# The second experts' rows in owner-sorted tiles of 128, with weights fetched by a register

## The reference, cut to what matters

```
x += norm(ssm + top1_experts(ssm))        # scan of 16 states; E=4 experts, 128 -> 512 -> 128, silu
x += cross_attention(norm(x), ctx)        # 256 queries, 256 keys per batch, one head of 128
# third block: top-2 of 8 experts, capacity 640 per expert
gates, idx = top_k(softmax(x @ wg), 2);  gates /= sum(gates)
loc  = cumsum(one_hot) - 1 (+ counts of first choices for second choices)
keep = loc < C;   pos = where(keep, idx * C + loc, E * C)
h = silu(disp @ fc1_w.T + fc1_b);  y = h @ fc2_w.T + fc2_b      # per expert
out = norm(x + gates[0] * y[pos0] + gates[1] * y[pos1]) * gamma + beta
```

## Time and profile before

| | |
|---|---|
| median of 3 runs | 476.78 us (476.72 to 478.07) |
| the profiled execution | 482.02 us |
| its span, first to last instruction | 480.2 us |
| mean granted TensorE clock | 0.885 |
| TensorE busy | 344.7 us (72% of the span) |
| VectorE, ScalarE, GpSimd busy | 292.0, 263.0, 230.6 us |
| DMA | 23.94 MB |

### The profile page before, as it was taken

One profiled execution on the slowest core, in us unless ns is written; L12 is line 12 of the kernel. 1 busy time (PEld: TensorE's weight loads), 2 busy tenths in 40 slices (PEclk: granted clock), 3 DMA queues, 4 the chain that ended last, 5 costly groups with the idle time before them and its releaser, 6 DMA issues. The chain is left out here.

```text
span 480.2 us, 5947 instructions
## 1 busy us (share of the span) xinstructions
PE 344.7 (72%) x1749; PEld 233.6 (49%) x1749; DVE 292.0 (61%) x840; ACT 263.0 (55%) x465; POOL 230.6 (48%) x275
## 2 busy tenths in 40 slices
PE   1427557769896899978999688661537789999460
PEld 0203333346464565645667455561327757767360
DVE  3478988956999799999974245357136012222055
ACT  3554645668887797868537675413224474554021
POOL 4425755543545665464541422716844435455434
PEclk9999965879999899999899988975558899999966
DMA  6999400000000000000000000200120221210243
GB/s 123 290 233 333 124 1 1 0 0 1 1 1 0 2 1 1 1 2 0 1 1 2 0 0 9 81 1 23 50 61 28 77 67 49 76 53 14 78 120 88
DMA packets 29472, 23.94 MB, mean 50 GB/s; under 512 B 5448, under 2 KB 23943, under 8 KB 29440
## 3 DMA queue, kind: packets, MB, share of 16 engines
q1 hardware_dynamic: 27048, 19.50, 14.8%
q0 software_dynamic: 2304, 4.04, 2.5%
q10 hardware_dynamic: 88, 0.03, 0.0%
HBM read 13.73 MB, written 10.52 MB: 51 GB/s over the span
## 5 line engine op out<-in xcount | busy, mean ns | idle before, releaser
L1072 POOL TENSOR_TENSOR yD<-yD,hc 128x512 f32<-128x512 f32 x64 | 84.4, 1318 | 103.5 <-DVE hc L537 97.9
L1398 PE MATMUL bank<-yD,w 128*128 128x512 f32 x128 | 71.9, 645 | 17.1 <-ACT hid L1202 16.2
L502 DVE TENSOR_TENSOR_SCAN h<-a,bank 128x512 f32<-128x512 f32 x64 | 77.8, 1216 | 1.4 <-DVE bank L489 0.5
L1407 PE MATMUL bank<-w,hid 128*128 128x128 f32 x512 | 74.6, 293 | 0.0
L1407 PEld LDWEIGHTS bank<-w,hid 128*128 128x128 f32 x512 | 68.6, 205 | 9.4 <-issue 6.1
L1389 PE MATMUL bank<-rows,selid 99*128 99x512 bf16 x128 | 47.5, 457 | 25.5 <-DVE hc L537 23.4
L1135 POOL DMA_INDIRECT y_rows<-yslot,dest x40 | 39.1, 977 | 37.6 <-DVE yslot L865 22.1
L1202 ACT ACTIVATE hid<-bank,cols 128x512 f32<-128x512 f32 x64 | 43.4, 683 | 18.0 <-PE bank L1398 11.9
L489 DVE TENSOR_TENSOR bank<-bank,u 128x512 f32<-128x512 f32 x64 | 43.8, 684 | 14.5 <-PE bank L1389 14.2
L1060 POOL DMA_INDIRECT slots_in<-xrow,posu x32 | 32.3, 1010 | 32.7 <-DVE locs L684 14.7
L1389 PEld LDWEIGHTS bank<-rows,selid 99*128 99x128 bf16 x128 | 12.8, 106 | 67.4 <-DVE hc L537 47.0
(11 more groups left out here) (235 smaller groups left out, 586.4 us busy)
## 6 DMA issues: line engine op xcount, KB each, us to landing
slots_in<-yslot SPq DMA_DIRECT2D x10, 258.0 KB, 6.3
xe_tok<-slots_in SPq DMA_DIRECT2D x8, 258.0 KB
y_rows<-yslot SPq DMA_DIRECT2D x8, 256.0 KB, 5.2
x_tok<-in_x_dram SPq DMA_DIRECT2D x4, 256.0 KB, 3.9
w<-in_L_attn_up_w_dram SPq DMA_DIRECT2D x1, 1024.0 KB
yD<-y_rows SPq DMA_DIRECT2D x4, 256.0 KB, 4.4
xT<-y_rows SPq DMA_DIRECT2D x4, 256.0 KB, 5.7
out_dram<-acc SPq DMA_DIRECT2D x4, 256.0 KB, 2.3
```

The source lines that it names most:

```text
L502: ins = v.tensor_tensor_scan(state_of(k), decay_of(k).rearrange("p j n -> p (j n)"), drive_of(k), 0.0, ALU.mult, ALU.add)
L1072: pool.tensor_tensor(grp(yD, g), grp(yD, g), read_of(k), ALU.add).then_inc(summed, 1)
L1398: pe.matmul(bank[UP_BANKS[f % 2]][:, 0:width(g)], w1[:, e, f * P:(f + 1) * P], grp(yD, g), start=True, stop=True).then_inc(up_ps, 1)
L1407: ins = pe.matmul(bank[DOWN_BANK][:, j * P:(j + 1) * P], hid[:, m % 2, f, j * P:(j + 1) * P], w2[:, e, f, :], start=(f == 0), stop=(f == F ...
```

## The change

The rows of the second experts no longer have fixed slots. They are sorted by expert into tiles of 128 rows, in three sets of tokens: token tiles 0 to 7, 8 to 11 and 12 to 15. A set of n token tiles has 2n + 7 row tiles, the most that eight experts can need, and all are computed: 23 + 15 + 15 = 53 row tiles. The first 38 run two per slot in slots 86 to 104, among the last group's attention steps; the last 15 after the slots.

- Weights: each expert's two transposed matrices are stored once to DRAM (`wts`, 8 x 512 KB, after they were turned at slot 14). For each row tile SyncE loads the owner's number into a register and fetches that owner's 512 KB into a ring of eight.
- VectorE: `seats` and `owners` work out where each expert's rows begin, and who owns each tile; `owners` also makes the tile's up bias. `take_in` copies four turned row tiles from PSUM to SBUF, `take_out` their four products. `combine` adds the two gated rows to the sum.
- GpSimd: 16 sends for the first set (slots 76 to 83), 8 for the second (slots 87 to 90), 8 for the third, after the slots; then 32 indirect gathers take each token's two result rows (`fetch`), of which the first eight stand at slot 99. The 40 sends to `y_rows` are gone.
- TensorE: per row tile one turn, four up products, one product over eight rows that adds the down bias of the owner, four down products. The gated sum is gone. ScalarE: four silus of 128x128 per tile.
- The loads of rows (`rows_in`), of weights and the stores of results (`rows_out`) are one queue of issues on SyncE, in the order that the diff shows.

```diff
+STAGES = 3
+BOUNDS = (0, 8, 12, TILES)
+MTS = [2 * (BOUNDS[s + 1] - BOUNDS[s]) + E2 - 1 for s in range(STAGES)]
+FFN_TILES = sum(MTS)
...
+W_RING = 8
+ROW_RING = 6
+Y_RING = 2
...
+FFN_SLOT = NS * G + 22
+FFN_PACE = 2
+def ffn_at(k):
+    n = FFN_PACE * (k - FFN_SLOT)
+    return [t for t in range(n, n + FFN_PACE) if 0 <= t < FIRST_TILE[-1]]
+def turns_at(k):
+    return [chunk_of(t) for t in ffn_at(k + 1) if t == chunk_tiles(chunk_of(t))[0]]
+def leaves_at(k):
+    return [chunk_of(t - 1) for t in ffn_at(k - 1) if t and t - 1 == chunk_tiles(chunk_of(t - 1))[-1]]
+FETCH_SLOT = FFN_SLOT + 13
...
+            def seats(g):
+                first, end = counted(g).start, counted(g).stop
+                square = [P, E2, E2]
+                link(v.tensor_tensor(firsts[:], off[:, end, 0, :], off[:, first, 0, :], ALU.subtract))
+                link(v.tensor_tensor(count2[:], off[:, end, 1, :], off[:, first, 1, :], ALU.subtract))
+                link(v.tensor_tensor(count2[:], count2[:], firsts[:], ALU.add))
+                link(v.tensor_tensor(full[:], count2[:].unsqueeze(2).to_broadcast(square),
+                                     rows128[:].unsqueeze(1).to_broadcast(square), ALU.is_gt))
+                link(v.tensor_reduce(tiles2[:], full[:], AX.X, ALU.add))
+                link(v.tensor_tensor(full[:], below[:], tiles2[:].unsqueeze(1).to_broadcast(square), ALU.mult))
+                link(v.tensor_reduce(lead2[:], full[:], AX.X, ALU.add))
+                for r in range(2):
+                    do(v.scalar_tensor_tensor(seat[:, r, :], lead2[:], float(P), off[:, first, r, :],
+                                              ALU.mult, ALU.subtract))
+                v.wait_ge(dve_done, n[0])
+                do(v.tensor_tensor(seat[:, 1, :], seat[:, 1, :], firsts[:], ALU.add))
+            def owners(s):
+                m = MTS[s]
+                mine = slice(FIRST_TILE[s], FIRST_TILE[s] + m)
+                wide = [P, m, E2]
+                link(v.tensor_tensor(past2[:], lead2[:], tiles2[:], ALU.add))
+                link(v.tensor_tensor(whose[:, 0:m, :], iota24[:, 0:m].unsqueeze(2).to_broadcast(wide),
+                                     past2[:].unsqueeze(1).to_broadcast(wide), ALU.is_ge))
...
+                link(v.tensor_copy(owner_no[:, mine], owner[0:1, 0:m]))
+                at["owner", s] = n[0]
+                do(v.tensor_scalar(owner_col[:, mine], owner[0:E2, 0:m], part_no[0:E2, 0:1], None, ALU.is_equal))
+                link(v.tensor_tensor(whose[:, 0:m, :], owner[:, 0:m].unsqueeze(2).to_broadcast(wide),
+                                     iota8.unsqueeze(1).to_broadcast(wide), ALU.is_equal))
+                link(v.tensor_tensor(bias_of[:, 0:m, :, :], whose[:, 0:m, :].unsqueeze(2).to_broadcast([P, m, FT, E2]),
+                                     cols[:, C_FCB:C_FCB + E2 * FT].rearrange("p (e f) -> p f e", f=FT)
+                                     .unsqueeze(1).to_broadcast([P, m, FT, E2]), ALU.mult))
+                link(v.tensor_reduce(up_bias[:, mine, :], bias_of[:, 0:m, :, :], AX.X, ALU.add))
+                at["up_bias", s] = n[0]
...
+            def take_in(c):
+                tiles = chunk_tiles(c)
+                v.wait_ge(xs_ps, c + 1)
+                if tiles[-1] >= XS_RING:
+                    v.wait_ge(up2_ps, tiles[-1] - XS_RING + 1)
+                for lo, hi in ring_runs(tiles, XS_RING):
...
+                at["xsT", c] = n[0]
+            def take_out(c):
+                tiles = chunk_tiles(c)
+                v.wait_ge(dn2_ps, tiles[-1] + 1)
+                if c >= Y_RING:
+                    v.wait_ge(st_y[c % Y_RING], 16 * (c // Y_RING))
+                else:
+                    v.wait_ge(zeroed, 16 * N_ZERO)
+                do(v.tensor_copy(yst[:, c % Y_RING, 0:len(tiles), :],
+                                 tiles3(bank[DOWN2_BANKS[c % 2]][:, 0:len(tiles) * P])))
+                at["yst", c] = n[0]
...
+            def combine(q):
+                v.wait_ge(acc_done, q + 1)
+                for i in range(q * GT, (q + 1) * GT):
+                    v.wait_ge(fetched[i], 32)
+                    for r, t in enumerate((first_y, second_y)):
+                        link(v.scalar_tensor_tensor(acc[:, i, :], t[:, i, :], g2[:, i, r:r + 1], acc[:, i, :],
+                                                    ALU.mult, ALU.add))
+                ln_stats(acc, quads(q), q, 4)
...
+            last = range(FIRST_CHUNK[-1], FIRST_CHUNK[-1] + CHUNKS[-1])
+            take_out(last[0] - 1)
+            combine(0)
+            take_in(last[0])
+            take_in(last[1])
+            combine(1)
+            take_in(last[2])
             finish(0)
-            sum_stats(3)
+            take_out(last[0])
+            take_in(last[3])
+            combine(2)
             finish(1)
+            take_out(last[1])
             finish(2)
+            take_out(last[2])
+            take_out(last[3])
             q = PG - 1
+            combine(q)
+            v.wait_ge(biased[3], G)
             for j in range(GT):
...
+            def weights(t):
+                r = t % W_RING
+                s = stage_of(t)
+                if t == FIRST_TILE[s]:
+                    sp.wait_ge(dve_done, at["owner", s])
+                if t == 0:
+                    sp.wait_ge(st_w, 16)
+                e = sp.value_load(owner_no[0:1, t:t + 1], min_val=0, max_val=E2 - 1)
+                if t >= W_RING:
+                    sp.wait_ge(dn2_ps, t - W_RING + 1)
+                load(wring[:, r, :], wts[bass.ds(e, 1), :, :].rearrange("e p n -> p (e n)"), ld_wt[r])
+            def rows_in(s):
+                sp.wait_ge(scattered[s], 16 * 2 * (BOUNDS[s + 1] - BOUNDS[s]))
+                for c in range(FIRST_CHUNK[s], FIRST_CHUNK[s] + CHUNKS[s]):
+                    tiles = chunk_tiles(c)
+                    first = tiles[0] - FIRST_TILE[s]
+                    if c >= ROW_RING:
+                        sp.wait_ge(xs_ps, c - ROW_RING + 1)
+                    load(xs_tok[:, c % ROW_RING, 0:len(tiles), :],
+                         srt[s][first * P:(first + len(tiles)) * P, :].rearrange("(j p) d -> p j d", p=P),
+                         ld_rows[c % ROW_RING])
+            def rows_out(c):
+                tiles = chunk_tiles(c)
...
+                sp.wait_ge(dve_done, at["yst", c])
+                load(ysrt[s][first * P:(first + len(tiles)) * P, :].rearrange("(j p) d -> p j d", p=P),
+                     yst[:, c % Y_RING, 0:len(tiles), :], st_y[c % Y_RING])
+            for t in range(FFN_TILES + W_RING):
+                if t == W_RING:
+                    sp.wait_ge(summed, UNITS)
+                    rows_in(0)
+                if t == FIRST_TILE[1] - 3:
+                    rows_in(1)
+                if t == FIRST_TILE[2]:
+                    rows_in(2)
+                if t < FFN_TILES:
+                    weights(t)
+                done = t - W_RING
+                if done >= 0 and done == chunk_tiles(chunk_of(done))[-1]:
+                    rows_out(chunk_of(done))
...
+            def fetch(q):
+                s = max(0, q - 1)
+                for b in range(Y_RING):
+                    mine = [c for c in range(FIRST_CHUNK[s] + CHUNKS[s]) if c % Y_RING == b]
+                    pool.wait_ge(st_y[b], 16 * len(mine))
+                for i in range(q * GT, (q + 1) * GT):
+                    for r, t in enumerate((first_y, second_y)):
+                        pool.indirect_dma_start(t[:, i, :], None, ysrt[s][:],
+                                                bass.IndirectOffsetOnAxis(ap=posu[:, r, i:i + 1], axis=0),
+                                                bounds_check=MTS[s] * P - 1,
+                                                oob_is_err=False).then_inc(fetched[i], 16)
...
+                for s, r, i in sends_at(k):
+                    dispatch(s, r, i)
+                if k == FETCH_SLOT:
+                    fetch(0)
+            for i in range(BOUNDS[-2], TILES):
+                for r in range(2):
+                    dispatch(STAGES - 1, r, i)
+            fetch(1)
+            inverse_root(quads(0), 0, 4)
+            fetch(2)
+            inverse_root(quads(1), 1, 4)
+            inverse_root(quads(2), 2, 4)
+            fetch(3)
+            inverse_root(quads(3), 3, 4)
...
+            def up2(t):
+                b = bank[UP_BANKS[t % 2]]
+                pe.wait_ge(dve_done, at["xsT", chunk_of(t)])
+                pe.wait_ge(ld_wt[t % W_RING], 16 * (t // W_RING + 1))
+                if t >= 2:
+                    pe.wait_ge(hid2_done, t - 1)
+                else:
+                    pe.wait_ge(hid_done, G * E1 * FT)
+                for f in range(FT):
+                    ins = pe.matmul(b[:, f * P:(f + 1) * P], wring[:, t % W_RING, f * P:(f + 1) * P],
+                                    xsT[:, t % XS_RING, :], start=True, stop=True)
+                ins.then_inc(up2_ps, 1)
+            def down2(t):
+                c = chunk_of(t)
```

(26 more changed lines are left out.)

574 lines of the change are left out of this document (179 added, 395 removed).

## The result

The changed kernel takes 525.27 us (median of 4 runs, 523.55 to 525.7) against 477.42 for the kernel before on the same chip (476.72 to 478.09): a ratio of 1.0996, interval 1.0963 to 1.1028. It is slower, as forecast, and 15 us beyond the forecast of 510, inside the range of 488 to 534. The profiled execution took 525.24, its span 523.5.

A forecast was written before the change was run, and what follows sets the result against it. TensorE was taken to bound the kernel outside a hole between two dense stretches. 320.5 + 116.1 (53 tiles) + 6.3 (attention) + 26.0 (tail) + 44.8 (waits) gave span 513.7, on the median 510; range 488 to 534.

The forecast's parts named there:

- The gap: TensorE idle before the third set's first tile, waiting for its rows: 12.0 us.
- The last set: The last 15 tiles, after the slots, with turns, half clock and ScalarE's normalizes: 37.0 us.
- The tail: From TensorE's last product to the end, take-out, store, gathers, gated adds, norm and stores: 26.0 us, against 33 before.
- the bias product: Per row tile on TensorE, the down bias over eight rows: 0.30 us of a 2.19 us tile.
- Steps 1 and 2: Slots 75 and 86: maximum of scores 6.3 us later; VectorE waits for rows, `add_expert` at 335.6, 15.1 us later.
- step 1: Slot 75: `seats` and `owners(0)` delay the last group's maximum by 6.3 us to 302.9, its normalize by 4.5.
- step 4: Tiles 0 to 37 with the attention's products, from 344.4 to 438.7 us: 87.3, plus 3.3 half clock and 3.7 silu stops.
- step 5: Third set after slot 101: counts, sends, loads and `combine(0)` bring its rows at 450.7; TensorE idles 12 us.
- (b): Rival: the first set's rows are in time, 10.6 us less, 500; 13 in 100.
- (c): Rival: the tiles fill TensorE from 325 on, waits under 11.3 us, time about 470; 5 in 100.
- X: All TensorE waits from 320.5 us on: 44.8 us forecast; the old time is met only at 11.3.
- step 6: The last 15 tiles, 37.0 us to 487.7, then 26.0 us to the end, span 513.7.

The follow-up runs named there:

- e2: Changed kernel with the bias product made over 128 rows, padded with zeros, instead of eight: 513.72 us.
- e1: Changed kernel without the bias product of the 53 tiles, so the output lacks that bias: 505.55 us.
- e6: Changed kernel with `owners(0)` and the rows' ranks in slots 75 and 76 moved behind the scores' maximum and the gates: 519.37 us.
- e5: e4 plus ten, not six, of the first set's sends ahead of group 2's root on GpSimd: 514.39 us.
- e4: Changed kernel with VectorE's first `take_in` moved behind the last `add_expert` and its statistics in slot 86: 524.78 us.
- e3: Changed kernel fetching only the first eight tiles' weights; the other 45 tiles compute with what lies in the ring: 525.81 us.
- e8: Changed kernel with the third set taken in before `combine(0)` and its rows loaded behind the weights of tiles 38 to 42: 519.26 us.
- e12: e10 at two tiles a slot as in the changed kernel, with SyncE's order of e8: 496.38 us.
- e10: Changed kernel with the edits of e2, e5 and e6, the third set taken in before `combine(0)`, and one tile a slot: 497.59 us, ratio 1.0444.
- e11: e10 with 40 row tiles instead of 53, losing some rows: 475.86 us, ratio 0.9982 to the kernel before.

## Why the prediction was right, and where its numbers were not

**Step by step in the span.** First down product: 344.4 forecast, 345.2 its bias product and 345.9 its first own record; I count 0.8. Tiles 0 to 37 with the attention: 94.3 forecast, 102.5 measured, +8.2. The gap: 12.0 and 11.8. The last set: 37.0 and 38.6, +1.6. The tail: 26.0 and 25.4, -0.6. Together 523.5 and not 513.7, +9.8. The other 5.2 of the 15 is in how I went from span to median: I took the kernel before as profiled 5.2 above its median (482.02 against 476.78) and subtracted as much; the changed kernel's profiled run lay on its median (525.24, 525.27).

**The term that was mis-sized is the bias product.** The forecast put 0.30 between 0.22 and 0.41. Measured are 0.41 and, in the eight records that follow, 0.20 that I had no term for. Both stood in the trace, and I did not see it. That trace has sixteen such pairs, not one, and at clock 1.00 the timeline of TensorE reads:

```profile
108.77 0.38 PE L1488 MATMUL bank<-ident,yD 128*128 128x128 f32 x2
109.09 0.48 PE L1490 MATMUL bank<-bias,gT 8*128 8x128 f32 x2
109.50 0.49 PE L1488 MATMUL bank<-ident,yD 128*128 128x128 f32 x2
109.92 0.48 PE L1490 MATMUL bank<-bias,gT 8*128 8x128 f32 x2
```

From start to start, a pair over eight rows takes 0.41 or 0.42, the ordinary pair ahead of the first 0.32, and the one between the two 0.42, where two ordinary records among their own kind take 0.22. So each change between 128 rows and eight costs the ordinary records some 0.10, which is the 0.20 per tile of the changed kernel. The 0.30 was a middle between two rows, of which one had the product's price.

0.31 in 53 tiles are 16.4 us, and only 9.8 show (8.2 and 1.6 above). That is luck: four smaller terms came out below the forecast, by 7 us together. The exponentials stopped the silus for 1.7 and 0.4 (forecast 2.5 and 1.2), the half clock cost 2.4 and 1.9 against the same records at full clock (3.3 and 3), the attention's own products took 4.8 (6.3), and the normalizes in the last set stopped nothing (2). e2 shows the cause by its form, e1 the whole price, and both that only 56 to 61% of it reaches the end.

**Steps 1 and 2 were right** within 2 us at each station (the maximum 304.1 for 302.9, normalize 315.7 for 313.8, the last send's end 330.5 for 328.9, `add_expert` 336.5 for 335.6). The one error of step 1 is `bias_of`, 1.41 us where its elements alone asked for 0.92. That is its own price: over 480 elements it took 1.00 with GpSimd idle (slot 86) and 1.02 beside a send. The send that started beside it took 1.71 and not 0.97, and in e6, which moves `bias_of`, the two sends that overlap it took 1.26 and 1.23. The gathers beside `combine`, which the sum left unchanged, were not slower: the one at 505.67, beside two gated adds, took 1.00. The sends did not run back to back from 299 to 329: six ended at 308.0, GpSimd then idled for 5.7 us, and ten more followed from 316.15 on, which is the pause that e5 fills. e5 shows the sends on the path by moving them; e6 shows it of VectorE's list only in direction. e4 shows the wait of `add_expert` right in place and in weight at the start (5.2 us), and that step 4 lacked a wait: behind an earlier start VectorE's list up to 350.3 holds tile 4 back, and the clock falls.

**The weights' traffic** is hidden, as said: TensorE does not wait for it inside the slots, and without it (e3) nothing is won. In step 5 it costs something. The Trainium skill's rule on transfers under load ("DMA: Bandwidth & Descriptors", section "Latency and other measured facts"), for which the forecast had a sentence of its own, shows in the changed kernel only in the store of 6.55 us, 2.6 beyond my 4; without the traffic (e3) it took 4.97. The rows' landing took 2.26, as before, for SyncE issues no weights from 429.7 until the rows have landed. Where it does (e8, e12), the landing took 6.02 and 6.35 us. That agrees with the rule in direction; the 4 us are more than the 2 us that the page gives for high load, as are the 6.3 against 2.3 that the forecast had already read the earlier trace rows. Rivals (b) and (c) did not come: the rows were late, and X is 40.3 with the measured prices (523.5 less 320.5, 53 tiles of 2.50, 4.8 of attention and the tail of 25.4), against 11.3.

**Step 5 was right in place and size,** and the experiments add what I had not said: from the counts to the first product is a chain of 32.4 to 33.0 us whatever a tile costs (changed kernel, e1, e2; 31.0 in e3, without the weights' traffic). Whoever speeds up the tiles lengthens the gap.

**Two slips that change nothing.** The hole of the earlier trace rows has three slices at a clock of 5 tenths, not four, and the terms of step 6's tail add up to 25.8, not 26.0.

**What made it slower at all.** The forecast named two things, 42 us of added TensorE time (now 53 x 2.50 - 74 = 58) and a start and a middle in which TensorE waits. e10 takes the dear part of the bias and a third of the waiting away (TensorE's waits from 320 on fall from 29.7 to 20.4 us), 27.7 us in all; e11 takes the 13 extra tiles, 21.7 us; with both the time is that of the kernel before. What stays open is the split between e10's forecast and its time: I named 10 us of it by TensorE's gaps, the rest lies in executions that differ by up to 8 us.

## What to carry to other kernels

A scheme that pads to an upper bound (2n + 7 tiles for 2n tiles of rows) is paid on the engine that bounds (here 1.67 of the 2.11 us of each extra tile); count the padded tiles first. When work is moved into an idle stretch, its price is also what it delays there: look at the in-order lists of the engines that feed the hole (GpSimd's sends, VectorE's copies) and move the transfers before the waits. And a gain upstream of a chain of fixed length between two bounded stretches comes out at the end only by the part that does not fall into the gap; take the chain out first, then speed up the work. e10 did both and still fell 13 us short of the sum, since one tile a slot uncovered the attention's waits; so look at what covered what before it is moved.
